# Two weight loads behind a value transfer in SyncE's order, and the condition products of the second pair on other banks

## What is computed

```
y   = einsum('bct,bcd->bdt', x, Wc[condition])      # per sample: 64 x 64 condition weight
qkv = y @ attn_qkvw + attn_qkvb                     # 1024 -> 3072
ctx = softmax(q k^T / sqrt(32)) v                   # 32 heads, sequences of 64
x   = x + ctx @ attn_ow + attn_ob
z   = x @ W.T + 2 * (top-2 of 8 experts, rank 16)   # condition layer 2
x   = x + ffn(z)                                    # quantized to 8 bit: gate, up, silu, down
```

## Time and profile before

| | us |
|---|---|
| median of 3 runs | 2176.74 (2173.77 to 2177.82) |
| the profiled execution | 2176.15, its span 2174.5 |
| PE busy | 2086.4 (96%) |
| GpSimd busy | 1395.3 (64%) |
| attention stage, about | 0 to 1186 of the span |
| PE in the stretch 60 to 1300 | 1193.3 of 1240 busy, clock granted 0.99 |
| GpSimd in the same stretch | 1018.8 of 1240 busy |

### The profile page before, as it was taken

How to read it: one execution, slowest core, us unless ns; L and a number is a source line. 1 busy time by engine, 2 the same in 40 slices (tenths; PEclk the granted TensorE clock), 3 DMA queues, 4 the chain that set the end, 5 groups by cost and what they waited for, 6 DMA issues and landing times.

```text
span 2174.5 us, 45944 instructions
## 1 busy us (share of the span) xinstructions
PE 2086.4 (96%) x18120; PEld 1698.1 (78%) x18120; DVE 1415.1 (65%) x2395; ACT 1044.2 (48%) x1364; POOL 1395.3 (64%) x1138
## 2 busy tenths in 40 slices
PE   6999999999999999899999899999999999999996
PEld 5878878788877888787887688888777877777784
DVE  5345565555564455644555865656688888888887
ACT  4355666556564556655565322123443444444343
POOL 6988888888888888788886810001355555455554
PEclk8999999999999999999999999999999999999998
DMA  3255554554544545545556355368444344344433
GB/s 122 65 119 112 120 141 107 117 121 106 136 123 103 122 104 122 137 93 126 109 123 202 118 174 188 121 199 237 115 112 102 96 116 106 93 109 111 103 85 97
DMA packets 413165, 267.05 MB, mean 123 GB/s; under 512 B 275778, under 2 KB 344514, under 8 KB 412482
## 3 DMA queue, kind: packets, MB, share of 16 engines
q1 hardware_dynamic: 410130, 261.38, 47.0%
q0 software_dynamic: 2864, 3.28, 0.9%
HBM read 152.92 MB, written 50.33 MB: 93 GB/s over the span
## 4 chain that ended last, share of the span: by engine, by line
PE 76%; POOL 10%; DMA 5%; DVE 4%; ACT 2%; issue 2%; SPq 1%; POOLq 0%; DVEq 0%; ACTq 0%
PE acc L811 30%; PE acc L1757 16%; PE acc L1225 6%; PE att L1225 6%; PE att L1784 5%; POOL w_slot_lo L401 5%; POOL w_raw L404 3%; PE att L1727 3%; PE acc L1793 2%; PE att L840 2%; POOL w_slot_hi L399 2%; DMA w_raw<-wu 2%; PE acc L1766 2%; PE att L867 2%; DMA x_raw<-x 1%
## 5 line engine op out<-in xcount | busy, mean ns | idle before, releaser
L811 PE MATMUL acc<-y_hi,w_slot_hi 128*128 128x512 f32 x1344 | 536.0, 399 | 29.5 <-ACT unit L538 16.6
L811 PE MATMUL acc<-y_lo,w_slot_hi 128*128 128x512 f32 x1344 | 528.0, 393 | 0.0
L811 PE MATMUL acc<-y_hi,w_slot_lo 128*128 128x512 f32 x1344 | 526.5, 392 | 0.0
L401 POOL TENSOR_TENSOR w_slot_lo<-w_raw,w_slot_hi 128x512 fp32r<-128x512 f32 x329 | 430.9, 1310 | 26.3
L811 PEld LDWEIGHTS acc<-y_hi,w_slot_hi 128*128 128x128 f32 x1344 | 254.7, 190 | 89.4 <-issue 17.7
L404 POOL TENSOR_TENSOR w_raw<-w_raw 128x512 f32<-128x512 f32 x188 | 255.5, 1359 | 77.8 <-DMA w_raw<-wu 73.4
L811 PEld LDWEIGHTS acc<-y_hi,w_slot_lo 128*128 128x128 f32 x1344 | 255.0, 190 | 54.6
L811 PEld LDWEIGHTS acc<-y_lo,w_slot_hi 128*128 128x128 f32 x1344 | 255.2, 190 | 50.2
L663 DVE TENSOR_TENSOR unit<-acc,unit 128x512 f32<-128x512 f32 x144 | 99.4, 691 | 236.4 <-PE acc L811 216.7
L632 DVE TENSOR_REDUCE top<-att 128x8 f32<-128x512 f32 x126 | 86.3, 685 | 251.0 <-PE att L840 245.9
L399 POOL CAST w_slot_hi<-w_raw 128x512 fp32r<-128x512 f32 x329 | 221.1, 672 | 24.2 <-PE acc L811 12.2
(11 more groups left out here) (184 smaller groups left out, 3966.5 us busy)
## 6 DMA issues: line engine op xcount, KB each, us to landing
w_raw<-wu SPq DMA_DIRECT2D x192, 256.0 KB, 3.2
c_raw<-context_T SPq DMA_DIRECT2D x16, 1024.0 KB, 6.2
f_x_all<-x_T SPq DMA_DIRECT2D x32, 512.0 KB, 4.9
f_xr_all<-x_T SPq DMA_DIRECT2D x32, 512.0 KB, 6.1
out<-f_raw SPq DMA_DIRECT2D x31, 512.0 KB, 3.4
context_T<-cx SPq DMA_DIRECT2D x60, 256.0 KB, 3.0
x_raw<-x SPq DMA_DIRECT2D x27, 512.0 KB, 4.3
xa<-xT SPq DMA_DIRECT2D x12, 1024.0 KB, 7.4
```

The source lines that it names most:

```text
L401: pool.tensor_tensor(w_lo[:, k], raw, w_hi[:, k].bitcast(F32), ALU.subtract).then_inc(w_set, 1)
L811: ins = pe.matmul(bank, w[:, k, c, :], v[:, k, c, :], start=(k in (0, 1, 5) and c == 0 and i == 0), stop=(c == C // 2 - 1 and i == 2), ski ...
```

## The change

Two edits. First, SyncE's loads of R12 and R22 for unit U + 1, which stood at the end of unit U - 1, now stand behind step 0 of unit U: behind that step's context store, its value transpose and its softmax transposes. In the first unit of a block they stay where they were, behind step 1. Second, the four results of the condition products are laid out in another order in their banks, Y12, Y22, Y11, Y21 in banks 0 to 3 (before Y12, Y11, Y22, Y21). The first tile of a pair now fills banks 2 and 3, so in the second pair of a later block only the second tile waits until the products' banks are evacuated. Since bank 1 now holds Y22, product 1 of a block's first unit waits for its last reader, the low part of product 3 on DVE.

```diff
-Y12, Y11, Y22, Y21 = 0, 1, 2, 3
+Y12, Y22, Y11, Y21 = 0, 1, 2, 3
...
                     elif k == 6 and U % UNITS == UNITS - 1:
                         for i in range(3, PAIRS):
                             load_x((r + 1) * PAIRS + i)
-                    elif k == 6:
-                        load_w(U + 2, R12)
-                        load_w(U + 2, R22)
-                    if k == 1 and U and U % UNITS == 0:
-                        load_w(U + 1, R12)
-                        load_w(U + 1, R22)
+                if U + 1 < ALL and U and k == (1 if U % UNITS == 0 else 0):
+                    load_w(U + 1, R12)
+                    load_w(U + 1, R22)
...
             if r and p == 0:
                 pe.wait_ge(sub_set, 2 * (4 * duos - 2))
                 pe.wait_ge(cx_set, 4 * duos - 4)
-            elif r and p == 1:
+            y_tile(r, 2 * p)
+            if r and p == 1:
                 pe.wait_ge(act_out, 4 * UNITS * r)
                 pe.wait_ge(dve_out, 3 * UNITS * r)
-            y_tile(r, 2 * p)
             y_tile(r, 2 * p + 1)
...
                 if k == 1:
-                    pe.wait_ge(t_raw, raw_at(3, PAIR * (r + 1)))
+                    pe.wait_ge(y_lo_dve, lo_at(3, PAIR * (r + 1)))
```

## The result

The changed kernel takes 2194.3 us as the median of 6 runs, the kernel before 2178.8 (6 runs, the 3 of the table above among them). The ratio is 1.0077, with a 95% interval of 1.0057 to 1.0098. The whole interval lies above 1, so the change makes the kernel slower. The forecast was 2165, faster; the range ended at 2174.5. The profiled execution took 2191.27 us, its span is 2189.6. That is 15.1 us over the span of before, and 14.5 of them are there when the output projection's first matmul starts (1201.41 in the place of 1186.87). So the attention stage lost it.

The account below looks back on a forecast made before the run. PE was taken to be the bound, stalled through ACT, the transpose, SyncE and GpSimd. -16.4 gross gain + 4.4 for GpSimd's lateness + 0.6 new wait = -11.4 us, from 2176.15 to 2165; range 2156 to 2174.5.

Parts of the forecast that it names:

- The chain: Attention stage: PE waits for ACT, transpose, SyncE and finally GpSimd; four stalls, one per block, 16.45 us together.
- the margin: GpSimd in the attention stage: 48.7 us of waits, 1.04 us per unit; using 27% takes 4.4 us off the gain.
- R22's lateness: GpSimd's slot 1 start: about 0.28 us later per unit, 0.12 from issue and 0.16 from landing.
- the late R22: Rival at GpSimd's slot 1: R22 0.85 us late per unit, 82% of the gain goes, 2174 us; 15%.
- The gross gain: PE's four stalls and the slow clock behind them: 16.4 us of at most 22.4 won by an earlier value transpose.
- new stalls in units 18, 21, 42 and 45: Sign on PE at L538, the evacuation of product 2: if stalls show in any of these units, the forecast is wrong.
- GpSimd's wait for R22: Sign in the attention stage: from 73.4 to 80 to 95 us; over 110 or over 130 points to a rival.
- the second rival: R22 lands late in two of three units, 0.85 us per unit; GpSimd's wait over 110 us, 2174 us; 15%.
- ACT's wait for vv: Sign on ACT, waiting for the value transpose: should fall from 68.6 to 30 to 45 us.
- The slower rival: Transposes ahead of R22 cost 1.32 us per unit, GpSimd sets the blocks' pace, 13 us longer, 2190 us; 8%.
- The banks: Second pair's first tile may start 1.45 us earlier, but gains nothing, hidden behind the next tile's wait for x.
- the new wait for DVE: Product 1 of a block's first unit: 0.3 us late with the semaphore, two places counted, 0.6 us.

Follow-up runs that it names:

- the swap: The kernel before, with GpSimd making slot 6 ahead of slot 5 and SyncE loading R22 ahead of R12: 2154.1 us, 0.9894.
- the extra cast: The kernel before, with GpSimd making slot 1's high part twice, one cast more per unit, transfer order untouched: 2193.4 us, 1.0075.

## Why the prediction was wrong

**The chain was read rightly, its limit was not.** PE waits for ACT, ACT for the value transpose, the transpose for SyncE, SyncE for GpSimd: that holds, and with GpSimd relieved nearly all of the stalls go (1.8 us are left with the swap). I took the upper link, SyncE's order, as the thing to mend. The lower one, GpSimd's pace, set the blocks' time, and the edit paid for the upper link with the lower.

**The failed step is the margin.** I counted 36.5 + 12.2 = 48.7 us as time by which GpSimd may be later at no cost, and by that put the point from which the change loses at 1.04 us per unit. The 36.5 us are waits for the condition products at the blocks' starts. They begin when PE gets there, and PE gets there when SyncE has brought x, which waits for GpSimd's slots: they move with the lateness and take up little of it (31.5 us were left, 30.5 with the extra cast). The 12.2 us of waiting for PE were a margin, 0.26 us per unit, and they were used up. The extra cast measures the margin without any transfer moved. The 47 casts, some 33 us of work, cost 15.7 us, so about half was taken up. That makes 0.4 us per unit, an estimate from this run, where I had 1.04. There is a flaw in the reasoning besides: I took the margin against PE as it stood, while a PE that is 16.4 us faster would leave GpSimd that much less.

**The second one is R22's lateness.** I took 0.28 us per unit; it was 29.3 / 47 = 0.62 by the waits, 0.70 by the means. Half of it is issue: R22 went 0.34 us after slot 6, not 0.12 + 0.03. Most of that is in the units with U mod 3 = 0, which I had priced at nothing: there R22 went 0.82 us after slot 6 on average and was late in 11 of 15 units, in the others 0.19 (U mod 3 = 1) and 0.03. I had counted 2.6 us for the issue of the two transposes; in unit 9 it was 1.46 + 2.76, and there was no time to spare. The other half is landing, 3.92 against 3.61 us, where I had 0.16; with U mod 3 = 0 it is 4.36 against 3.67. GpSimd's longer casts, 9.3 us, had no term at all. And one row was misread: I called the load issued at 377.4 one with no transpose near, but a value transpose went 0.4 us behind it (at 377.82), as behind that of unit 15.

The sum lay within the bounds that I wrote down (up to 0.92), and the price of 0.85 us per unit that I gave for the late R22 was a gain of 2.4 us only because of the false margin. With 0.26 us it would have read (0.62 - 0.26) x 47 = 17 us of loss; measured were 15. That closeness is partly luck, for the sum leaves out the longer casts.

**The gross gain, 16.4 us, came where it was looked for, and was lost elsewhere.** Unit 3 shows it best, for there the two kernels are within 0.4 us of each other. The transpose went at 106.84 in the place of 110.65, the stall of 2.67 us and the slow clock are gone, and the unit is 4.5 us shorter. After its data the transpose went 2.1, 5.5, 5.0 and 5.1 us later in units 3, 15, 27 and 39, before 6.3, 5.75, 8.0 and 8.0: 2.9 to 4.2 us less in three of the four, where 3.4 was forecast. In unit 15 nothing was won there, for R21 and the context store stand ahead and wait for GpSimd. The four units are 17.9 us shorter in all. How much of this in the later blocks comes of PE being late there anyway isn't separated. But a PE that gains on GpSimd has to wait for it elsewhere, and it did, in ten other units and at the blocks' starts.

Of the prediction's own signs, new stalls in units 18, 21, 42 and 45 came true, all four of them. GpSimd's wait for R22 (102.7 us) lay over the 80 to 95 of the forecast and under the 110 of the second rival, and ACT's wait for vv stayed at 65.8 where 30 to 45 was forecast. The slower rival had the right sign and nearly the size (2190) at 8%. That is luck in part: its price of 1.32 us per unit was twice what was measured, and its margin of 1.04 well over what there was.

**The banks** went as predicted: the tile's earlier start is hidden behind x (7.0 us of waits for x in the run with the banks alone), the new wait for DVE showed once, with 0.3 us, and the edit's effect can't be told from nothing (1.0003).

By the Trainium skill (DMA: Bandwidth & Descriptors, "Two DMAs through the same engine are not ordered") descriptors of one queue start in order on each DMA engine. The longer landings with transposes ahead (4.11 and 3.92 against 3.61 us) agree with it, though no run here shows that the order is their cause.

## What to carry over

An idle time of an engine is a margin only if it would not move when that engine comes later. Ask of each wait what releases it, and whether this hangs on the engine itself a few steps back; here three quarters of what I called margin did (36.5 of 48.7 us). When two engines run at nearly the same pace, price an edit on the one that has no time to spare, even if the stall shows on the other, and look first for the resource that is freed last: here two independent steps in the other order gave 24 us, while a reordered queue cost 15.

## What was new about the hardware

The issue of a DMA transpose of 128x1024 16-bit words on SyncE's queue took 1.24 to 1.27 us in the median, but over 2 us in 13 of 182 cases before and in 18 in the changed kernel, at most 3.0, and everything behind it on SyncE waited for that. What makes one long isn't shown: of 15 softmax transposes issued within 1.8 us of a value transpose in the changed kernel, the median took 1.42 us and two took over 2, among them the 2.76 of unit 9. A 256 KB load (R22) landed 0.3 to 0.5 us later on average in the kernels with transposes ahead of it in the queue. All six gaps of 5.2 to 5.9 us before a matmul, two before and four with the extra cast, were followed by a granted clock of 0.50. Of the 13 stalls of up to 3.1 us of the changed kernel 12 were followed by the full clock over 4 us, and the longest, of 3.06 us, by 0.57. The length of the gap alone does not tell: before, one of 2.67 us was followed by 0.68 over 4 us, and one of 3.18 us by 1.00.
